# Where ScalarE makes the decays of the next turn: behind the sixth Silu of a turn instead of behind the eighth

## The reference

```python
def _L1_attn_ref(x, A_log, B_mat, C_mat, D_vec, W_dt, b_dt):   # 16 states per channel
    A = -jnp.exp(A_log)
    dt = jax.nn.softplus(jnp.einsum('bth,gh->btg', u, W_dt) + b_dt)
    def step(state, inp):
        A_bar = jnp.exp(dtA * A)                       # the decays
        state = A_bar * state + dtA * B_mat * u_t[..., None]
        y_t = jnp.einsum('bhn,hn->bh', state, C_mat) + D_vec * u_t

def _L1_ffn_ref(x, router_w, router_b, w1, b1, w2, b2, sw1, sb1, sw2, sb2):
    # 64 experts of hidden width 32, weights cw from the top 8; two shared experts
    h = jax.nn.silu(xf @ W1 + B1) @ W2 + B2
    acc = acc + cw[:, None] * h

x = x + _L0_attn_ref(xn, ...) + _L0_ffn_ref(xn, ...)
x = x + _L1_attn_ref(xn, ...) + _L1_ffn_ref(xn, ...)
```

## Time and profile before

| | |
|---|---|
| median of three runs | 524.03 us (523.99 to 524.27) |
| the profiled execution's own time | 524.22 us |
| its span in the profile | 522.4 us |
| busy: PE, DVE, ACT, POOL | 442.2, 382.8, 278.1, 194.8 us |
| granted TensorE clock, mean | 0.952 |
| second layer's turns | from about 364 to 507 us |

### The profile page before, as it was taken

The page is one execution under the profiler, slowest core; times in us unless marked ns, Lnnn a source line. Parts: engine busy times, 40 slices in busy tenths (PEclk is TensorE's granted clock), DMA queues, the critical chain, the costliest instruction groups (busy, mean ns, idle before and its releaser), DMA issues.

```text
span 522.4 us, 7319 instructions
## 1 busy us (share of the span) xinstructions
PE 442.2 (85%) x2143; PEld 325.9 (62%) x2143; DVE 382.8 (73%) x702; ACT 278.1 (53%) x392; POOL 194.8 (37%) x188
## 2 busy tenths in 40 slices
PE   2729999999999999999989969299689778977893
PEld 1327887888878888788877845155455445544452
DVE  5687478944888448894498987776768877887784
ACT  2375674426644275533655255835676577557730
POOL 1248014400144001530002100740477778777850
PEclk9958999999999999999999979579799999999997
DMA  6420001100012000000000000000265776687664
GB/s 177 96 61 23 2 0 43 43 1 0 0 41 52 0 0 0 0 0 0 1 0 2 1 0 1 0 2 0 55 130 114 144 141 131 116 157 137 126 130 120
DMA packets 29535, 26.76 MB, mean 51 GB/s; under 512 B 10837, under 2 KB 25414, under 8 KB 29510
## 3 DMA queue, kind: packets, MB, share of 16 engines
q0 software_dynamic: 4608, 16.78, 16.8%
q1 hardware_dynamic: 24902, 9.69, 7.3%
HBM read 8.64 MB, written 1.05 MB: 19 GB/s over the span
## 4 chain that ended last, share of the span: by engine, by line
PE 29%; DVE 28%; POOL 19%; issue 13%; ACT 7%; DMA 2%; DVEq 1%; SPq 0%; POOLq 0%; ACTq 0%
POOL state L435 9%; PE psum L1083 7%; PE psum L203 6%; PE psum L205 6%; PE psum L204 6%; POOL xn_tok L439 4%; POOL g_hi L448 3%; DVE hid L771 2%; PE psum L1203 2%; DVE at_m L800 1%; DVE at_m L802 1%; POOL g_lo L449 1%; DVE xn_tok L693 1%; POOL sel_now L450 1%; PE psum L1218 1%
## 5 line engine op out<-in xcount | busy, mean ns | idle before, releaser
L567 ACT ACTIVATE sil<-psum 128x512 f32<-128x512 f32 (+1 forms) x96 | 56.3, 596 | 104.3 <-PE psum L205 91.2
L771 DVE TENSOR_TENSOR hid<-sil,psum 128x512 f32<-128x512 f32 (+1 forms) x96 | 65.1, 686 | 51.8 <-PE psum L205 32.9
L1083 PEld LDWEIGHTS psum<-e_w,hid 128*128 128x128 f32 (+1 forms) x768 | 94.9, 191 | 6.0
L1083 PE MATMUL psum<-e_w,hid 128*128 128x128 f32 (+1 forms) x768 | 95.3, 274 | 0.0
L203 PE MATMUL psum<-xn_hi,e_hi 128*128 128x512 f32 (+1 forms) x192 | 81.8, 426 | 7.9 <-DVE hid L771 7.3
L975 DVE TENSOR_TENSOR_SCAN state<-dec,win_t 128x1024 f32<-128x1024 f32 x32 | 73.4, 2295 | 20.0 <-ACT dec L643 20.0
L205 PE MATMUL psum<-xn_lo,e_hi 128*128 128x512 f32 (+1 forms) x192 | 76.0, 396 | 0.0
L204 PE MATMUL psum<-xn_hi,e_lo 128*128 128x512 f32 (+1 forms) x192 | 75.8, 395 | 0.0
L652 ACT ACTIVATE sil<-psum,vec_t 128x512 f32<-128x512 f32 x64 | 43.2, 687 | 47.3 <-PE psum L205 36.8
L435 POOL TENSOR_SCALAR state<-state,ssm_cb 128x1024 f32<-128x1024 f32 x32 | 49.7, 1552 | 45.2 <-DVE state L975 42.2
L1258 PE MATMUL psum<-hid,g_w 128*128 128x512 f32 x128 | 61.3, 592 | 0.0
(11 more groups left out here) (261 smaller groups left out, 766.5 us busy)
## 6 DMA issues: line engine op xcount, KB each, us to landing
xn_tok<-state POOLq DMA_DIRECT2D x32, 512.0 KB, 4.5
e_raw<-in_L_ffn_w SPq DMA_DIRECT2D x16, 128.0 KB, 2.1
e_raw<-in_L_ffn_w SPq DMA_DIRECT2D x8, 176.0 KB, 2.4
res<-in_L_attn_x SPq DMA_DIRECT2D x4, 256.0 KB, 3.9
g_raw<-in_L_ffn_w SPq DMA_DIRECT2D x16, 64.0 KB, 2.3
g_w<-in_L_ffn_w SPq DMA_DIRECT2D x16, 64.0 KB, 2.5
out<-res SPq DMA_DIRECT2D x4, 256.0 KB, 2.9
e_raw<-in_L_ffn_w SPq DMA_DIRECT2D x16, 48.0 KB, 1.9
```

Source lines behind the costliest of these rows:

```text
L567: act.activation(sil[0:M, s % 2, :], ps[s % 2][0:M, :], ACT.Silu).then_inc(silu_done, 1)
L771: dve.tensor_tensor(hid[0:M, tb % 2, ft, :], sil[0:M, s % 2, :], ps[2 + s % 2][0:M, :], ALU.mult).then_inc(gated, 1)
L1083: ins = pe.matmul(ps[4 + o % 2][:, n * P:(n + 1) * P], hid[0:m, tb % 2, ft, n * P:(n + 1) * P], e_w2[j][0:m, ft, :], start=(ft == 0), stop ...
```

## The change

ScalarE's loop over the turns makes the two decays of the next turn behind the sixth Silu of a turn (s = 5) and then the seventh and eighth Silu; before, it made them behind the eighth. No instruction is added or dropped, and the other engines' programs are the same.

```diff
             for i in range(NG // GPI):
-                for c in range(i * GSTEPS, (i + 1) * GSTEPS):
-                    silu(c)
-                if i < NG // GPI - 1:
-                    for j in range(GPI):
-                        decay((i + 1) * GPI + j)
+                for s in range(GSTEPS):
+                    silu(i * GSTEPS + s)
+                    if s == GSTEPS - 3 and i < NG // GPI - 1:
+                        for j in range(GPI):
+                            decay((i + 1) * GPI + j)
```

## The result

The changed kernel takes 537.16 us (median of four runs, 535.45 to 538.28) against 524.15 us of the kernel before: a ratio of 1.0242, 95% interval 1.0209 to 1.0275. It is 13.0 us slower; 537.8 was forecast. The profiled execution took 535.45 us with a span of 533.6 us, the shortest of the four, and had the highest mean granted clock of them, 0.938 against 0.926 to 0.930.

A forecast was written before the change was run, and what follows sets the result against it. A chain changing engines, with no engine full, was taken to set the 17.70 us turn. 524.22 + 1.5 (chain and last turn) + 12.3 (clock falls) = 538.0 us, 537.8 as median; range 526.5 to 543.5.

The forecast's parts named there:

- Steps 1 and 2: Per turn: VectorE's 3.76 us of waits go, but return before the seventh Silu, where PE stands still 3.34 us.
- Step 3: In each turn, four second products of PE stand exposed after the seventh Silu: 17.88 us against 17.70, seven times +1.3.
- rival (c): Clock holds, but POOL's scale holds the shared port 0.9 us at scan 1: seven times 0.45, 528.7 us; 4%.
- The further 0.2 us for the last turn: Last turn's scan 3 starts 1.3 us behind a Silu's end instead of 1.1: +0.2 us once, at the end.
- Step 4: SP's queue: later weight loads cost nothing, as POOL's split in the next turn leaves at least 0.4 us of cover.
- Step 5: PE's 3.34 us gap drops TensorE's clock to 0.50 in six of seven turns, 2.0 us each: 12.3 us.
- (b): TensorE's clock holds at 1.00 through all the gaps: 525.5 us, range 524.5 to 527; 11%.
- Rival (d): The decays' order matters to nothing: VectorE's 3.8 us change place and PE catches up, 524.0 us; 3%.
- Rival (a): Faster: VectorE's chain sets the turn, a period of 15.95 us, seven times -1.75, 512.0 us; 4%.

The follow-up runs named there:

- the fillers: Changed kernel, with PE also issuing ten zero-weight matmuls that add nothing in its gap in each of the seven turns: 527.19 us, ratio 1.0054.

## Why the prediction was right, point by point

Steps 1 and 2 held within 0.3 us: the decays' wait is gone from the seven turns, PE's gap was forecast at 3.34 us and is 3.2 to 3.4, VectorE's 3.8 and is 3.5 to 3.85. The 2 us that I had left for the first turn's wait were too few: that wait was 5.0 us in the kernel before (20.0 less 15.0 in the seven turns) and is 6.1 now. No term of the sum rests on it.

Step 3, PE's order as the new chain: shown by the run that changes nothing but that order (525.03 us) and by the one that changes only VectorE's (538.64, and 18.27 in its turn without a fall). The size was 0.32 too small: 18.20 us a turn without a fall, not 17.88, so 3.5 us in all and not 1.3. The term that was missing is rival (c), as far as the timelines show: I gave the port 4% as a case of its own, while it takes part in the likeliest case, with 0.6 us of delay to the scan instead of my 0.9 and about 0.3 us to the turn instead of 0.45. It does so in the three turns without a fall; in those with one, no scan 1 takes over 2.33 us. The further 0.2 us for the last turn did not show: the last turn's scan 3 starts 11.2 us later than before, no more than the seven turns make.

Step 4 held in its sum, not in its cover: the first weights came too late for POOL's split in two turns, which cost POOL 2.1 us of waiting in all, and the list of waits has no other engine waiting for POOL. In the first of these turns SP issued them at E+13.8, as walked (13.7), but POOL had them only 4.4 us later, not 2.3:

```profile
POOL g_hi L448 <- DMA g_raw<-in_L_ffn_w: 2.1, 2, 1.1
```

Step 5, the clock: shown by the fillers, which take away most of the gap, leave no fall and bring 10 us back, of which about 1.8 are the chain's and not the clock's. I had six falls at 2.0 us, 12.3 us; the profiled execution had four at 1.9 on average (two at 1.4 and two at 2.4 to 2.6, near the ends of 1.6 and 2.5 that I had named), 7.7 us. The medians are 13.0 us apart, which leaves about 9.5 us for the clock if the chain's 3.5 are the same in each run. So that the sum came within 0.6 us of the median is luck: the clock's term was some 3 us too large and the chain's some 2 us too small. Against the profiled execution alone, 538.0 was 2.5 us too much. One sum in the recorded text is off: four falls at 1.6 us end at about 532 us, not at 530. A count of falls can't be had from the trace of before; the range had to hold it, and did.

Rivals (b) and (c) needed a clock that holds. With the fillers it does, at 527.19 us, between their 525.5 and 528.7. Rival (d) needed PE to catch up, and it did not.

Rival (a), faster, needed in(10) ahead of the outs. With two of four outs moved, PE stood aside and VectorE's chain came forward, and it gave no gain until scan 0 was moved too, then POOL until its copies were gone. At each step what ended second took over.

## What to carry to other kernels

A block that keeps one engine busy is free only for what the other engines have queued under it, in their order: here four matmul groups on PE that had been under the block of decays stood behind it after the move, though each single wait looked shorter. Count, for the new place, which instructions of each engine's queue can run before the block's result is needed, and what is left behind it. And when a move joins PE's short gaps into a longer one (here the clock fell with gaps of 2.5 us and more, and held with 1.2 and 1.7), price the clock with it. A run with filler matmuls that add zero tells about how much of a loss is the clock's; read its turns against turns without a fall, since fillers can also shift what meets what, which made 1.8 of the 10 us here.

## What the runs showed of the hardware that I had not expected

The number of falls grew with the gap, but with no sharp edge: none of seven turns at gaps of 1.2 and of 1.7 us, four at 2.5 us, four and six at 3.4 us (two kernels with the same gap), seven at 4.1 us. A fall need not come inside the gap that brings it: in one turn PE stood still until 446.11, was at work again for a microsecond at 1.00, and then ran at 0.50 for 3.4 us.

```profile
446.20:447.10 0.90, 0.90 (x4) 0.69 (x5) 0.90 (x2) 0.36 (x2) 0.82 (x3) 1.00 0.98 187
447.20:450.40 3.20, 3.20 (x7) 1.88 (x6) 2.46 (x2) 1.25 (x2) 2.92 (x3) 0.50 0.85 164
```

The plain fp32 matmuls of L1258 slow down at 0.50 as well: the eight of the outs, part of them at 0.50, took 4.25 us up to the next L203, against 3.03 in a turn at 1.00.
